# A two-layer spectral block: the T transpose written to layer 1's second bank, and placed ahead of the second forward-W pair

## What is computed

```python
# layer 0
f  = fft2(x, norm='ortho');  Xh = (f.real - f.imag)[:, :, :46]        # kept: 23 kw, all 45 h
o1 = relu(einsum(Xk, w1[0]) + b1[0]);  o2 = einsum(o1, w2[0]) + b2[0] # 8 blocks of 48 channels
x  = ifft2(softshrink(o2, 0.01)).real + x
# layer 1
xf = rfft2(x);  xr, xi = its real and imaginary part                  # kept: 23 kw, all h
o1r = relu(xr@w1[0] - xi@w1[1] + b1[0]);   o1i = relu(xi@w1[0] + xr@w1[1] + b1[1])
o2r = softshrink(o1r@w2[0] - o1i@w2[1] + b2[0]);  o2i = softshrink(o1i@w2[0] + o1r@w2[1] + b2[1])
y  = irfft2(o2r + 1j*o2i) + x
```

## Time and profile before

| | us |
|---|---|
| median of 3 runs | 517.57 (516.96 to 521.88) |
| the profiled execution | 518.28 |
| its span, first to last instruction | 516.5 |
| PE busy in the span | 482.8 (93%) |
| mean granted TensorE clock | 0.984 of full |

### The profile page before, as it was taken

The page is one execution under the profiler, slowest core; times in us unless marked ns, Lnnn a source line. Parts: engine busy times, 40 slices in busy tenths (PEclk is TensorE's granted clock), DMA queues, the critical chain, the costliest instruction groups (busy, mean ns, idle before and its releaser), DMA issues.

```text
span 516.5 us, 14950 instructions
## 1 busy us (share of the span) xinstructions
PE 482.8 (93%) x6192; PEld 341.7 (66%) x6192; DVE 307.6 (60%) x674; ACT 208.8 (40%) x473; POOL 172.4 (33%) x194
## 2 busy tenths in 40 slices
PE   4979999999999999999999999999999999998773
PEld 1347777676776777767777777767777677876521
DVE  6634465457745676447754677466764577566643
ACT  0025544543444434643355443554354433534201
POOL 9823222223341343213441144213351123222124
PEclk9999999999999999999999999999999999999967
DMA  9999763868889688886899678876889665634397
GB/s 211 262 253 279 203 178 95 179 178 207 251 212 230 171 229 252 193 218 182 256 231 227 177 202 260 233 206 184 267 211 248 165 173 163 146 92 134 110 256 227
DMA packets 77256, 105.25 MB, mean 204 GB/s; under 512 B 7584, under 2 KB 63666, under 8 KB 77190
## 3 DMA queue, kind: packets, MB, share of 16 engines
q1 hardware_dynamic: 57606, 56.74, 41.6%
q0 software_dynamic: 10608, 40.66, 29.5%
q10 hardware_dynamic: 8976, 6.90, 5.7%
HBM read 52.84 MB, written 51.43 MB: 202 GB/s over the span
## 4 chain that ended last, share of the span: by engine, by line
PE 72%; DMA 9%; DVE 7%; POOL 3%; SPq 3%; issue 3%; ACT 2%; POOLq 0%; ACTq 0%
PE ps L657 14%; PE ps L725 12%; PE ps L750 11%; PE ps L712 10%; PE ps L622 9%; PE ps L670 7%; PE ps L737 4%; DMA scr_i<-et 4%; DMA scr_f<-fs 4%; PE ps L688 4%; PE ps L698 2%; DVE img L587 2%; SPq L364 2%; POOL xs L407 2%; DVE ns L561 2%
## 5 line engine op out<-in xcount | busy, mean ns | idle before, releaser
L587 DVE TENSOR_TENSOR img<-ps,img 90x768 f32<-90x768 f32 x92 | 82.6, 900 | 21.7 <-PE ps L657 18.1
L407 POOL TENSOR_TENSOR xs<-xs,nt 128x360 f32<-128x360 f32 (+1 forms) x48 | 41.5, 865 | 146.3 <-DVE nt L539 120.5
L657 PE MATMUL ps<-jr,cst 64*90 64x384 f32 (+1 forms) x358 | 81.7, 526 | 7.7 <-DVE img L587 5.4
L416 POOL DMA_DIRECT2D y<-img x42 | 34.7, 826 | 133.8 <-DVE img L587 133.4
L622 PE MATMUL ps<-img,cst 128*64 128x384 f32 (+1 forms) x368 | 72.5, 510 | 7.2 <-DMA img<-x 6.4
L471 ACT ACTIVATE o<-ps,wt 97x180 f32<-97x180 f32 (+1 forms) x96 | 33.8, 406 | 104.6 <-PE ps L712 104.6
L561 DVE SCALAR_TENSOR_TENSOR ns<-p,ps 109x384 f32<-109x384 f32 x96 | 53.1, 553 | 37.7 <-ACT p L478 32.8
L725 PE MATMUL ps<-wt,o 128*64 128x96 f32 x1472 | 73.9, 249 | 0.1
L725 PEld LDWEIGHTS ps<-wt,o 128*64 128x64 f32 x1472 | 64.9, 137 | 12.3 <-issue 12.3
L712 PE MATMUL ps<-xs,wt 64*97 64x180 f32 (+1 forms) x768 | 68.0, 313 | 3.9 <-POOL xs L407 3.5
L750 PE MATMUL ps<-ns,cst 64*90 64x192 f32 x736 | 71.0, 322 | 0.0
(11 more groups left out here) (43 smaller groups left out, 413.6 us busy)
## 6 DMA issues: line engine op xcount, KB each, us to landing
y<-img POOLq DMA_DIRECT2D x35, 540.0 KB, 5.7
img<-x POOLq DMA_DIRECT2D x25, 540.0 KB, 8.5
scr_i<-et SPq DMA_DIRECT2D x48, 270.0 KB, 5.8
scr_f<-fs SPq DMA_DIRECT2D x154, 72.0 KB, 3.2
bt<-scr_f SPq DMA_DIRECT2D x40, 270.0 KB, 5.0
jr<-scr_i SPq DMA_DIRECT2D x48, 216.0 KB, 5.2
img<-x ACTq DMA_DIRECT2D x10, 576.0 KB, 8.5
y<-img SPq DMA_DIRECT2D x11, 270.0 KB, 3.3
```

Of the source, the lines that this page charges most:

```text
L407: nc.gpsimd.tensor_tensor(re, re, nt[s % 2][:, :, 0:kws(s), 0:H], ALU.subtract).then_inc(re_ok, 1)
L587: nc.vector.tensor_tensor(y, p, y, ALU.add).then_inc(i_add, 1)
L657: last = mm(ps[0:W, B0 + r, 0:n], K["w_inv"][64 * r:64 * r + 64, :], set_rows(t, j)[64 * r:64 * r + 64, at, 0:n], start=True, stop=True)
```

## The change

T now writes P2 + 1, the second bank of layer 1, which c1 and d1 use, instead of P1. Four waits follow from that. T waits for `d1_ss` of its own step alone, no longer for `d0_ss` of the next step. c0 no longer waits for `t_add`. c1(s) waits for `t_add` of T(s-1), the T that stands just ahead of it. The order list also moves T: in steps without inv groups it stands ahead of the second pair of fwd groups, in the others where it stood.

```diff
@@ schedule()
-        order += fwd[s][2:4]
+        t_ = [("t", s - 1)] if 0 < s <= NSTEPS else []
+        order += (fwd[s][2:4] + t_ if inv[s] else t_ + fwd[s][2:4])
         if s < 2:
             order.append(("x", 2 * s + 2))
-        if 0 < s <= NSTEPS:
-            order.append(("t", s - 1))
         order += inv[s][2:3]
@@ vector, kind "t"
-                        nc.vector.tensor_tensor(v, ps[0:rows, P1, 256 * p:256 * p + 256]...
+                        nc.vector.tensor_tensor(v, ps[0:rows, P2 + 1, 256 * p:256 * p + 256]...
@@ tensor, kind "c0"
                     if s > 0:
                         pe.wait_ge(d0_ss, 2 * s)
-                    if s > 1:
-                        pe.wait_ge(t_add, 2 * s - 2)
@@ tensor, kind "c1"
                     if s > 0:
                         pe.wait_ge(d1_ss, 2 * s)
+                        pe.wait_ge(t_add, 2 * s)
@@ tensor, kind "t"
                     pe.wait_ge(d1_ss, 2 * s + 2)
-                    if s + 1 < NT:
-                        pe.wait_ge(d0_ss, 2 * s + 4)
...
-                            last = nc.tensor.transpose(ps[0:rows, P1, 256 * p + 128 * q:256 * p + 128 * q + 128],
+                            last = nc.tensor.transpose(ps[0:rows, P2 + 1, 256 * p + 128 * q:256 * p + 128 * q + 128],
```

More of the change, by code:

```diff
@@ L568, in _ @@
                         v = ns[0:rows, p, :, 0, :]
-                        nc.vector.tensor_tensor(v, ps[0:rows, P1, 256 * p:256 * p + 256].rearrange("p (n c) -> p n c", c=64)[:, :, 0:BS], v, ALU.add).then_inc(t_add, 1)
+                        nc.vector.tensor_tensor(v, ps[0:rows, P2 + 1, 256 * p:256 * p + 256].rearrange("p (n c) -> p n c", c=64)[:, :, 0:BS], v, ALU.add).then_inc(t_add, 1)
                 if kind == "e":
```

## The result

The changed kernel takes 521.88 us (median of 19 runs, 519.54 to 524.21), the kernel before 517.45 (19 runs, 514.58 to 521.88). The ratio is 1.0087 with a 95% interval of 1.0071 to 1.0103: 0.9% slower, 4.4 us, against a forecast of 1.0% and 5.05 us.

A forecast was written before the change was run, and what follows sets the result against it. PE, busy 93% of the span, was taken as the bound. Terms 1.15 + 3.7 + 0.9 - 1.1 + 0.1 + 0.3 = 5.05 us slower took 518.28 to 523.3 us (profiled execution), range 519.2 to 526.4.

The forecast's parts named there:

- The largest term: Eight steps where c1 follows T at once: c1 waits for the adds behind T, together 3.7 us slower.
- step 5: One step where c1 follows T at once: c1's load starts at 77.70 against 76.92, 0.78 us later.
- The moved T: 15 steps with fwd and no inv: a third change of tile shape exposes a fwd load, 0.15 a step, 2.25 us.
- What is taken up of it: Inv's waits for ACT's copies of fwd, in i = 3 steps of some tasks, absorb 1.1 us, leaving 1.15.
- i = 0: Six steps with inv: c1's load goes 0.16 us later, passed on in five or six, 0.9 us slower.
- i = 4: Six steps with inv: T no longer waits for layer 0's shrink, 0.18 us gained each, -1.1 us.
- i = 5: Six steps with inv: c1 later, but inv's wait for DVE's add covers it; zero in five, 0.1 in one.
- i = 3: Six steps with fwd and inv: c1's block ends 0.13 later, partly covered; 0.05 each, 0.3 us slower.
- Rival 3: T's freedom from layer 0's shrink is the whole effect, adds never delay c1: 2 us faster, 515.6; chance 0.06.
- Rival 2: No cover holds and every release by DVE costs PE a queue refill: 9 us slower, 526.6; chance 0.18.
- Rival 1: Waits for inv adds, copies and POOL's xs cover more delays, moved T's cost nothing: 2.5 us, 520.1; chance 0.24.
- What the changed profile would show: In PE's waits, a new c1 entry for DVE's adds, 3 to 5 us on products; T's layer 0 shrink entry gone.

The follow-up runs named there:

- The third bank: The changed kernel, but the eight T that c1 follows at once write fwd's first bank: 517.57 us, against 517.17 for the kernel before, ratio 1.0021.

## Why the prediction was right

- **The largest term**, c1 held by the adds with nothing between, 3.7 us: 3.48 in seven steps and 0.26 in the eighth. The third bank took out exactly this. The 0.12 from the end of an add to PE's load, read off the inv groups, was measured as 0.11 and 0.12 here, and the product starts another 0.03 behind, which is why the last task's steps are 0.63 longer, not 0.60, and step 5 0.81, not 0.78.
- **The moved T**, 0.15 a step for the third change of shape: 0.15 in eleven of eleven. In these traces the load of fwd starts 0.08 ahead of its product behind a block of the same shape, and with its product, 0.00 ahead, behind T. Of the two pages of the Trainium skill, "TensorEngine Tiling (Array Packing)", Key Properties, has the engine drained at a change of tiling mode, and "TensorE: Matmul & The Clock Gate", Step-by-step, has weight loads pulled ahead of products in flight. The trace agrees with the second while the shape stays and with the first where it changes.
- **What is taken up of it**, 1.1 us: this was misread. I read three waits in one trace as a property of the kernel. They hang on when stores have landed, and two executions of the kernel before differ there by 1.46 us. The sum of the four steps against the trace of before was -1.76 in one trace of the changed kernel and -0.17 in the other, with -0.5 forecast. Their moved T would have added 0.6, so 2.4 and 0.8 us were taken up; that the 1.1 lies between is luck.
- **i = 0**, 0.9: 0.81, and the one step in which POOL's xs is later shows 0.0, as said.
- **i = 4**, -1.1 by a choice between 0.06 and 0.27 a step: -0.18 a step, in both traces and with the bank changed in these steps alone.
- **i = 5**, no fixed cost: the cover by the inv add held (1.92 us from adds to inv before and after, and 0.00 in four of the six stretches). **i = 3**, 0.3: 0.12, the cover there was nearly whole.
- **Rivals.** Rival 3, faster, needed the adds to be over before c1's load; they ended after it in every uncovered step. Rival 2's refill is the 0.03 above. Rival 1's covers at the uncovered steps do not exist.
- **What the changed profile would show**: one number missed. c1's new wait was said to be 3 to 5 us and is 8.0. The view books an idle stretch whole to the releaser that came last, so it took over the idle time that had been POOL's, too.
- **What can be told apart.** The prediction took 1% as about the least that a measurement can tell from none. With 19 runs of each the interval is 0.16% to either side, so 0.9% is clear of zero.

What repeats in both traces makes 5.25 us (1.66 + 3.48 + 0.26 + 0.81 - 1.08 + 0.12), against 4.4 and 5.1 us between the medians. The steps that vary took 1.04 off in the first trace and 0.03 in the second, so they can explain the difference, but no run shows that they do so in the medians: the steps i = 4 alone, above, are a case in which 1.1 us of repeating steps isn't found there. The mechanism and the terms that repeat were thus right one by one, the waits were not; that the sum of 5.05 came within 0.7 us of the median is in part luck.

## What to carry to other kernels

When a buffer is moved to another owner's bank, the wait moves with it: write down for each place what stands between the producer and the new waiter, and price the places where nothing does, since a few of these can hold most of the loss (8 of 48 here, 3.7 us). A block placed as a cover has to fit the tile shape of its neighbours, or one more weight load is in the open, 0.15 us a step here. And a wait that hangs on DMA should be read from two executions before it is counted as cover.

## What the runs showed that was not expected

- The steps that PE, DVE and ACT set repeat to 0.01 or 0.02 us between executions and even between kernels, so a change can be read in them to a hundredth or two, far below the 0.2 to 0.5% (1 to 2.5 us) to which the timed runs tell kernels apart.
- Six steps of 0.18 us gained at i = 4 did not show in the medians (ratio 1.0012, 0.9986 to 1.0037).
- Near the start of the kernel, in two of the nine traces, the granted clock fell to 0.50 (1.2 GHz) for 3.4 us after PE had stood idle for 2.0 and 2.1 us ahead of the first c1, and that cost 1.2 to 1.4 us, several times what a moved T costs.
- T between fwd and inv covers about 0.6 us a step of ACT's copies, four times what a change of tile shape costs.
